# Cross-attention and quantised feed-forward: row sums added in two DMA chains, row maxima eight rows ahead, pair additions in two halves

## The reference

```python
xn = layer_norm(_layernorm(x), g1, b1);  cn = layer_norm(context, g2, b2)
q, k, v = xn @ Wq.T, cn @ Wk.T, cn @ Wv.T          # split into 16 heads of 32
scores = einsum('bqhs,bkhs->bhqk', q, k) / sqrt(32)  # masked with -inf
attn = softmax(scores, axis=-1)                     # over 2048 context rows
x = x + einsum('bhqk,bkhs->bqhs', attn, v) @ Wo.T + bo
z = _layernorm(x)                                   # then FP6 blocks of 32:
x = x + dequant(fp6(z)) @ dequant(fp6(weight)).T + bias
```

## Time and profile before

| | |
|---|---|
| time, median of 3 runs | 5028.72 us (5018.85 to 5039.0) |
| the profiled execution | 5029.38 us, span 5027.6 us |
| mean granted TensorE clock | 0.98 |
| busy share of the span | PE 93%, DVE 68%, ACT 57%, POOL 55% |

### The profile page before, as it was taken

The page is one execution under the profiler, slowest core; times in us unless marked ns, Lnnn a source line. Parts: engine busy times, 40 slices in busy tenths (PEclk is TensorE's granted clock), DMA queues, the critical chain, the costliest instruction groups (busy, mean ns, idle before and its releaser), DMA issues.

```text
span 5027.6 us, 65944 instructions
## 1 busy us (share of the span) xinstructions
PE 4669.9 (93%) x25616; PEld 1361.6 (27%) x25616; DVE 3425.6 (68%) x3983; ACT 2841.1 (57%) x5128; POOL 2761.9 (55%) x1218
## 2 busy tenths in 40 slices
PE   4999989998999989999899998999989999899998
PEld 2322242222422224222242222422224222242223
DVE  4688557885578855788557885568845788457883
ACT  3477634775347753477544774457744577446773
POOL 2267643676437663376633766346763467525665
PEclk9999999999999999999999999999999999999999
DMA  5223432234323343232432324323343223342232
GB/s 180 64 60 68 108 111 62 60 69 122 98 55 63 65 124 100 51 68 59 126 100 57 68 60 120 104 50 68 64 118 107 54 60 68 115 113 54 59 68 71
DMA packets 173787, 413.38 MB, mean 82 GB/s; under 512 B 26833, under 2 KB 100881, under 8 KB 146594
## 3 DMA queue, kind: packets, MB, share of 16 engines
q0 software_dynamic: 27648, 201.34, 19.9%
q1 hardware_dynamic: 145826, 207.83, 13.5%
HBM read 110.98 MB, written 21.01 MB: 26 GB/s over the span
## 4 chain that ended last, share of the span: by engine, by line
PE 73%; SPq 7%; DVE 6%; ACT 5%; DMA 4%; POOL 3%; issue 2%; ACTq 0%; DVEq 0%; POOLq 0%
PE banks L912 18%; PE banks L922 18%; PE banks L830 11%; PE banks L890 9%; PE banks L824 8%; PE banks L946 7%; SPq L286 4%; DVE max_parts L553 3%; ACT region L713 3%; SPq L312 3%; DMA queries_stacked<-max_rows 2%; PE banks L799 2%; POOL wkT_wvT_wqT L391 1%; DVE queries_stacked L578 1%; DMA region<-in_x 1%
## 5 line engine op out<-in xcount | busy, mean ns | idle before, releaser
L553 DVE TENSOR_REDUCE max_parts<-banks 128x2 f32<-128x1024 f32 x2048 | 2410.7, 1220 | 594.1 <-PE banks L890 592.0
L713 ACT ACTIVATE region<-banks 128x512 f32<-128x512 f32 x4096 | 2214.8, 595 | 830.5 <-PE banks L912 790.0
L391 POOL TENSOR_TENSOR wkT_wvT_wqT<-region 128x2048 f32<-128x2048 f32 x320 | 1474.6, 4608 | 1273.8 <-ACT region L713 1158.1
L912 PE MATMUL banks<-queries_stacked,keys_stacked 98*128 98x512 f16 x4096 | 1262.3, 388 | 90.3 <-DMA queries_stacked<-max_rows 57.6
L922 PE MATMUL banks<-region,values 128*32 128x512 f32 x8192 | 1105.3, 612 | 7.6
L890 PE MATMUL banks<-keys_stacked,queries_stacked 33*128 33x512 f16 x4096 | 661.7, 386 | 41.9 <-DMA keys_stacked<-region 33.1
L912 PEld LDWEIGHTS banks<-queries_stacked,keys_stacked 98*128 98x128 f16 x4096 | 277.7, 97 | 1433.0 <-ACT region L713 1262.4
L830 PE MATMUL banks<-region,wkT_wvT_wqT 128*128 128x512 f16 x2304 | 565.1, 386 | 50.4 <-POOL region L374 23.5
L571 DVE RECIPROCAL row_sums_inverse<-row_sums_inverse 128x128 f32<-128x128 f32 x256 | 235.3, 935 | 401.4 <-ACT row_sums_inverse L730 401.4
L544 DVE SCALAR_TENSOR_TENSOR region<-banks,region 128x512 f16<-128x512 f32 x192 | 132.5, 690 | 369.0 <-ACT region L698 368.1
L830 PE MATMUL banks<-wkT_wvT_wqT,region 128*128 128x512 f16 x1536 | 378.4, 390 | 1.2 <-DVE region L544 1.2
(11 more groups left out here) (77 smaller groups left out, 2793.0 us busy)
## 6 DMA issues: line engine op xcount, KB each, us to landing
wkT_wvT_wqT<-wkT_wvT_wqT POOLq DMA_DIRECT2D x128, 1024.0 KB, 7.0
wkT_wvT_wqT<-sums POOLq DMA_DIRECT2D x64, 1024.0 KB, 7.0
keys_stacked<-region SPq DMA_DIRECT2D x768, 64.0 KB, 2.0
region<-in_x SPq DMA_DIRECT2D x24, 1024.0 KB, 7.8
wkT_wvT_wqT<-weights_split SPq DMA_DIRECT2D x8, 3072.0 KB, 18.2
queries_stacked<-region SPq DMA_DIRECT2D x384, 64.0 KB, 2.0
region<-in_context SPq DMA_DIRECT2D x16, 1024.0 KB, 6.3
values<-in_context SPq DMA_DIRECT2D x16, 1024.0 KB, 6.0
```

The lines of the kernel that those rows point to most:

```text
L391: e.tensor_tensor(SUMS[dst], PR[i], PR[i + 1], ALU.add).then_inc(s_pr, 1)
L553: e.tensor_reduce(mpart[:, buf, :, a, t, c], MXB[parity], AX.X, ALU.max).then_inc(s_mxd, 1)
L713: e.activation(PR[u % 4][:, j * HALF:j * HALF + HALF], score_bank(kt, j)[0], ACT.Exp, scale=SCALE).then_inc(s_ex, 1)
L912: e.matmul(dst, KA[0:STR, ds(ka + (j * C + (u + 1) * P), P)], QA[0:STR, ds(qa[j], HALF)], start=True, stop=True).then_inc(s_st, 1)
```

## The change

- **Two chains.** The first chain adds pairs 1, 2, 3 onto pair 0 as before, but the buffers change their parts from unit to unit (`buffers`). A second chain adds pairs 5 and 6 onto pair 4 in `SUMS[4]` with two more DMAs (`merge_late`, semaphore `s_ac2`). In the last unit of a batch the second chain is left out.
- **Four row sums a unit** in place of six: `PR[2]` in step 15, and in the next unit `PR[3]` in step 0, the first chain in step 2, the second in step 5. The last unit has all six of its sources in step 15. ACT's copy of `LB` moves from tile 5 to tile 7, and three score banks are used from tile 8 on instead of from tile 6; there is no return to two banks at tile 15, but tile 0 has two.
- **Maxima eight rows ahead.** `HEAD` has eight rows of unit 1 instead of four, 48 half rows instead of 40, in the last 18 front entries instead of the last 16. The maxima are complete after step 7, the transposition stands inside step 9 and uses bank 4, and rows 8 to 15 of a unit are made one unit earlier.
- **Pairs in two halves.** Each addition on POOL is two instructions of 1024 columns; ACT waits for the half it needs.
- SP starts the load of the feed-forward weights one step later, directly before the loads of `x`.

```diff
-    HEAD = [(r, 0) for r in range(16)] + [(r, 1) for r in range(12, 16)]
-    DURING = dict(zip(FRONT[-16:], [3, 3, 3, 3] + [3, 3, 2, 0] + [3, 3, 3, 3] + [3, 3, 2, 0]))
+    HEAD = [(r, 0) for r in range(16)] + [(r, 1) for r in range(8, 16)]
+    NHEAD = len(HEAD)
+    DURING = dict(zip(FRONT[-18:], [2, 2] + [3, 3, 3, 3] + [3, 3, 2, 0] + [3, 3, 3, 3] + [3, 3, 3, 3]))
...
         def score_bank(tile, j):
-            if 6 <= tile < KT - 1:
-                return bank((7, 4, 5)[(4 * (tile - 6) + j) % 3]), 3
-            return bank(4 + j % 2), 2
+            if tile < 8:
+                return bank(4 + j % 2), 2
+            slot = 4 * (tile - 8) + j + ((tile, j) >= (10, 2))
+            return bank((7, 4, 5)[slot % 3]), 2 if tile == 10 and j >= 2 else 3
+        def buffers(n):
+            return [(0, 1, 2, 3, 4), (3, 1, 0, 2, 4), (2, 1, 3, 0, 4)][n % 3]
...
# SP
-                e.wait_ge(s_pv, b * (NU * KT) + NU * KT + 3)
+                e.wait_ge(s_pv, b * (NU * KT) + NU * KT + 4)
                 e.dma_start(SUMS[4], wd_dram).then_inc(s_fl, 16)
-                e.wait_ge(s_pv, b * (NU * KT) + NU * KT + 4)
                 for h in range(2):
                     e.dma_start(X1[:, 4 * h:4 * h + 4, :], xb[:, h]).then_inc(s_xl[h], 16)
...
# POOL
                         def pair(p, dst):
-                            e.wait_ge(s_ex, n * (KT * J) + (2 * p + 2) * J + 2)
                             i = 2 * (p % 2)
-                            e.tensor_tensor(SUMS[dst], PR[i], PR[i + 1], ALU.add).then_inc(s_pr, 1)
+                            for h in range(2):
+                                half = ds(2 * HALF * h, 2 * HALF)
+                                e.wait_ge(s_ex, n * (KT * J) + (2 * p + 1) * J + 2 * h + 4)
+                                e.tensor_tensor(SUMS[dst][:, half], PR[i][:, half], PR[i + 1][:, half],
+                                                ALU.add).then_inc(s_pr, 1)
+                        def merge_late(i, p, src):
+                            e.wait_ge(s_pr, n * 14 + 2 + 2 * (p + 1))
+                            if i > 0:
+                                e.wait_ge(s_ac2, (late + i) * 16)
+                            e.dma_start(SUMS[second], SUMS[src], accum_op=ALU.add).then_inc(s_ac2, 16)
...
+                        pair(0, first)
+                        if g + q > 0:
+                            e.wait_ge(s_ac2, (late - 1) * 16)
+                        pair(1, one)
+                        merge(0, 1, one)
+                        e.wait_ge(s_pv, n * KT + 4 + 3)
+                        pair(2, two)
+                        if g + q > 0:
+                            e.wait_ge(s_ac2, late * 16)
+                        pair(3, three)
+                        merge(1, 2, two)
+                        e.wait_ge(s_pv, n * KT + 4 + 6)
...
+                        pair(4, second)
+                        e.wait_ge(s_acc, (3 * n + 1) * 16)
+                        pair(5, one)
+                        merge(2, 3, three)
+                        if not end:
+                            merge_late(0, 5, one)
+                        pair(6, two)
+                        if not end:
+                            merge_late(1, 6, two)
...
# DVE, unit(g, q, last)
-                    for k in range(1, J - 1):
+                    if not end:
                         for t in range(QT):
-                            if not end:
-                                max_row(idx + 8 * k + 2 * t, 1 - q, k * QT + t)
-                            if last and k == J - 2:
-                                invert(m - 1, t)
-                        if last and k == J - 2:
-                            normalise(m - 1, n - 1)
-                    if not end:
-                        maxima(1 - q, n + 1, idx + 8 * (J - 1))
+                            max_row(idx + 8 + 2 * t, 1 - q, QT + t)
+                        maxima(1 - q, n + 1, idx + 16)
+                    if last:
+                        for t in range(QT):
+                            invert(m - 1, t)
+                        normalise(m - 1, n - 1)
                     if not last:
                         for t in range(QT):
-                            max_row(idx + 8 * (J - 1) + 2 * t, q, (J - 1) * QT + t)
+                            max_row(idx + 16 + 2 * t, q, 2 * QT + t)
+                        for t in range(QT):
+                            max_row(idx + 24 + 2 * t, q, 3 * QT + t)
                             if n > 0 and t >= 2:
                                 invert(m - 1, t - 2)
...
# ACT, unit(g, q, last)
-                            exps(m, g, kt // 4, kt % 4,
-                                 (lambda: row_sums(m - 1, KT + 4)) if kt == 5 and n > 0 else None)
...
+                            if kt == 7 and n > 0:
+                                halfway = lambda: row_sums(m - 1, KT + 6)
+                            if kt == 10 and not end:
+                                halfway = turned
+                            exps(m, g, kt // 4, kt % 4, halfway)
...
# PE, unit(g, q, last)
+                            if g + q > 0:
+                                if t == 0:
+                                    sums = [(PR[3], None)]
+                                if t == 2:
+                                    sums = [(SUMS[buffers(2 * g + q - 1)[0]], (s_acc, 48 * m))]
+                                if t == 5:
+                                    sums = [(SUMS[4], (s_ac2, 16 * (b * (2 * NU - 2) + 2 * (2 * g + q))))]
+                            step(m, ex, ka, qa, v, u, t + 1, rows[u], sums=sums, closing=t == 5,
+                                 between=(lambda: turn_next(ex)) if t == 9 and not end else None, turning=not end)
...
+                    quad(0, *at(0, 0, ng, nq, not end))
+                    quad(1, *at(1, 1, ng, nq, not end))
+                    quad(2, *at(2, 2, g + 1, q, not last))
                     ex, ka, v, rows = at(K3, J - 1, g + 1, q, not last)
```

More of the change, by code:

```diff
@@ L205, in build @@
         s_acc = sem("pairs_merged")
+        s_ac2 = sem("late_pairs_merged")
         s_po = sem("unit_outputs_done")
@@ L395, in merge @@
+                        first, one, two, three, second = buffers(2 * g + q)
+                        end = g == G - 1 and q == 1
+                        late = b * (2 * NU - 2) + 2 * (2 * g + q)
                         def merge(i, p, src):
-                            e.wait_ge(s_pr, n * 7 + 2 + p + 1)
+                            e.wait_ge(s_pr, n * 14 + 2 + 2 * (p + 1))
                             if i > 0:
                                 e.wait_ge(s_acc, (3 * n + i) * 16)
-                            e.dma_start(SUMS[here], SUMS[src], accum_op=ALU.add).then_inc(s_acc, 16)
@@ L403, in _ @@
-                        e.wait_ge(s_pv, n * KT + (3 if g + q > 0 else 4))
-                        pair(0, here)
-                        e.wait_ge(s_pv, n * KT + 4 + 2)
-                        pair(1, other)
-                        merge(0, 1, other)
-                        e.wait_ge(s_pv, n * KT + 4 + 4)
-                        pair(2, 2)
+                            e.dma_start(SUMS[first], SUMS[src], accum_op=ALU.add).then_inc(s_acc, 16)
+                        def merge_late(i, p, src):
+                            e.wait_ge(s_pr, n * 14 + 2 + 2 * (p + 1))
+                            if i > 0:
+                                e.wait_ge(s_ac2, (late + i) * 16)
+                            e.dma_start(SUMS[second], SUMS[src], accum_op=ALU.add).then_inc(s_ac2, 16)
@@ L410, in _ @@
+                        e.wait_ge(s_pv, n * KT + 4)
                         if n > 0:
                             e.wait_ge(s_acc, 3 * n * 16)
-                        pair(3, 3)
-                        merge(1, 2, 2)
-                        pair(4, other)
+                        pair(0, first)
[4 more added lines that the diff above has]
+                        e.wait_ge(s_pv, n * KT + 4 + 3)
@@ L909, in score @@
                             e.wait_ge(s_ex, ex + (u + 1) * J + j + 3 - back)
-                            if back == 3 and tile == 6 and j == 0:
+                            if tile == 8 and j == 0:
                                 e.wait_ge(s_on, m + 1)
+                            if tile == 11 and j == 0 and turning:
+                                e.wait_ge(s_mc, m + 2)
                             e.matmul(dst, KA[0:STR, ds(ka + (j * C + (u + 1) * P), P)],
@@ L932, in step @@
                             mm.then_inc(s_po, 1)
+                    if between:
+                        between()
                     score(2)
@@ L948, in step @@
                     mm.then_inc(s_pv, 1)
-                    if between:
-                        between()
                 def clear(bank, left, count):
@@ L982, in unit @@
                     clear(OB, s_oc, m + 1)
-                    quad(0, *at(0, 0, ng, nq, not end), *([[[c] for c in late(m - 1)]] if g + q > 0 else []))
-                    for k in range(1, K3):
```

(25 more changed lines are left out.)

69 lines of the change are left out of this document (34 added, 35 removed).

## The result

The changed kernel (called *after* below, the kernel before it *before*) took 5114.0 us (median of four runs, 5102.1 to 5127.0) against 5032.2 for before on the same chip: ratio 1.0166, 95% interval 1.0132 to 1.0201. It is slower by 1.7%; 4998 was forecast, 5042 was the upper end of the range. The profiled execution has a span of 5100.2 us, 72.6 above before's.

The account below looks back on a forecast made before the run. PE bounds the kernel, holding 73% of the span. Per batch -7.5 (units 1 to 5) - 1.4 (unit 0) - 7.1 (unit 6) + 1.5 (unit 7) + 3.0 (tail) + 7.6 (front) = -3.9, times eight -31: 4998 us, range 4936 to 5042.

Parts of the forecast that it names:

- The step that failed: POOL and new DMAs: pair 0 starts about 2 us late behind the second chain's transfers, priced at nothing.
- Rival 2: POOL's two halves hold DVE out as one; normalise 2.9 us late, 2.2 more in four units a batch: 5068; chance 0.09.
- Rival 3: Second chain lands late, PE's step 5 waits some 7 us in 48 units: +330, 5330; chance 0.03.
- Rivals 1 and 4: Rival 1: front not held up, 4934, chance 0.18; rival 4: no change, bounds met at upper ends, 5018, chance 0.13.
- unit 1, -1.78: Units 1 to 5, each: two row-sum sources -1.98, maxima wait -0.96, two-bank steps +1.16; bounds -2.94 and -1.2.
- the +0.35 for a late `normalise`: Units 2 to 5: normalise meets pair 1's first half, delaying row 2's reductions by 0.7, half covered; bounds 0 and 0.7.
- unit 6, -7.1: Unit 6: 54.50 us falls to 47.4, since maxima are joined after step 7; bounds -9 and -5.
- unit 7, +1.5: Unit 7: two row-sum sources moved behind the last outputs +1.0, two-bank steps +0.5; bounds 0 to 2.5.
- tail, +3.0: Tail: x becomes the second of two loads, behind the weights, and lands later; bounds 0 and 3.2.
- The front: Front: early reductions ahead of chunk 5's normalisation delay PE, +6.3, low clock +1.7, sum +7.6; bounds +4.5 and +10.
- -0.4 for the end of the front: Front's end: four more pairs hide the 1.43 wait and add 0.4 net; less low clock at unit 0, -0.8.
- The gain of 0.8 at unit 0's start: With the idle before unit 0 gone, its low clock may stay away: -0.8, half of 1.7.

Follow-up runs that it names:

- the kernel with the multiplication first: Changed kernel with GpSimd waiting for VectorE's normalise multiplication (of two units before) ahead of pair 1, except in unit 2: 5020.1 us, ratio to before 0.9981.
- the run with whole pairs: Changed kernel with each pair of tiles added in one POOL instruction again instead of two halves: 5098.7 us (one run).
- the kernels with the front's and with the tail's edit: Changed kernel with the last chunk normalised ahead of the early reductions: 5066.6 us; changed kernel with x loaded ahead of the feed-forward weights: 5097.9 us.

## Why the prediction was wrong

**The step that failed** is this one: "Pair 0 of the next unit starts behind that queue, about 2 us late, and ACT needs its buffers only in step 3. Cost nothing; without that cover every us of lateness is one us of PE in 48 units." Pair 0 was late by about that (2.1 us more in the long one of the two units shown), and in the kernel with the multiplication first POOL was as late and the units that have the wait took 47.2 to 47.4, so ACT had its buffers. But the price named one user of POOL's time and left out the other. The forecast let `normalise` meet the first half of pair 1 alone, with pair 1 starting when ACT has its exponentials ready; with pair 0 late, pair 1 is ready when pair 0 ends, and DVE waits for both halves. That cost 5.7 us in 15 units, 86 us. Without it after would have come out near 5028, within half a per cent of before and inside the range; the front's 2.4 us a batch over its forecast are 19 of the 30 that then remain.

**Rival 2** had the mechanism ("it decides once POOL's second half is queued before the first ends") and was given 0.09. It was dismissed by the earlier trace rows, where DVE was through at once between two POOL operations. There the next operation began 0.04 us before the last one ended; in the long units it is 0.3. The row didn't show the case in question. Its price was too low (2.2 a unit: the clock was left out, and it takes two halves, not one), its number too high (32 units; 15 met it).

The Trainium skill's rule that was cited (SBUF — State Buffer, section Who interferes with whom: whole instructions exclude each other, issue order decides) agrees with the rows in part: DVE gets in at a boundary between two additions only where the second hasn't begun yet. The longest that the runs show of this is 18 us (below).

**Rival 3** did not come: the first late merges took 11.4 to 13.8 us in place of 7.0, and PE never waited for them. **Rivals 1 and 4** fall with the front and the long units.

**What was right, step by step** (us a batch, predicted and measured against before, long units aside): unit 1, -1.78 and 49.3 to 47.4 = -1.9; units 2 to 5, -1.43 each and 49.3 (their median before) to 47.83 = -1.5; the +0.35 for a late `normalise` in it, and 0.33 by the run with whole pairs; unit 0, -1.4 and -1.5; unit 6, -7.1 and 54.4 (its median before) to 47.7 = -6.7; unit 7, +1.5 and +1.9; tail, +3.0 and +2.7.

**The front** was right in its mechanism and short in its size: +7.6 forecast, +10.0 measured. The hold-up with its clock was put at 8.0, and undoing it gave back 6.3. What remains over before is 3.7, where the forecast had -0.4 for the end of the front. Eight pairs more stand in a front, at 0.39 us 3.1 of these; the forecast counted the four at its end at 0.4 net of a hidden wait. PE's wait for the stacked copies grew a little (4.84 at 826.08, 4.05 in the earlier trace rows; 36.8 in all, 33.1 in before), and the clock is low behind it (0.50 from 827 to 831; 0.57 from 804 to 808 in the earlier trace rows). How the 3.7 divide among these was not tested. The gain of 0.8 at unit 0's start was not found.

**Open**: what makes the first late merge land later in 15 of 40 units than in the other 25, at the same place in the code. In the 15 it lands 6.07 us or more after the unit's first score, in the 25 at most 5.88. It isn't chance: all 15 are long again in the kernels with the front's and with the tail's edit (17 and 16 long units). The trace has a companion, transfers of 8 or 16 KB on the DMA queues that the page calls `instruction` (packets, MB, share of 16 engines):

```profile
q8 instruction: 195, 3.19, 0.3%
q14 instruction: 121, 0.99, 0.1%
```

Between the issue of the first chain's last merge and the landing of the first late one, such a transfer runs in all 15 long units and in 16 of the others; the nine merges without one land within 11.37 to 11.41 us, those with one in 11.36 to 13.76. That these transfers are the cause was not tested. What is shown, by the merge sent 2.3 us earlier, is that the overlap of the two merges makes up most of what the late one takes beyond 7.0 (8.5 in place of 11.4).

## What to carry to other kernels

When an engine's work is shifted by a stated time, price it for every engine that shares something with it, not only for the one that waits on its result: here 2 us on GpSimd were free for ScalarE and cost 86 us by way of a multiplication of 0.69 us on VectorE. Look for such short instructions that must fall into a gap of another engine, and make the gap by a semaphore (0.74 us of GpSimd's idle time) rather than leave it to timing. In a unit mean that moves little, look for two populations before pricing anything by the mean.

## What was unexpected of the hardware

A VectorE multiplication can be shut out by a row of GpSimd instructions as long as each begins before the last one ends. Timeline of after, unit 7 of the third batch: it lasts from 1855.57 to 1873.63, through additions and DMA issues. There are two such in after, and they cost nothing: unit 7 takes 51.68 us in all eight batches. The kernel in which each half waits for the last one has none of these.

```profile
1855.57 18.06 DVE L604 TENSOR_TENSOR queries_stacked<-queries_stacked,row_sums_inverse 128x512 f32<-128x512 f32 x1
1857.02 1.18 POOL L410 DMA_DIRECT2D sums<-wkT_wvT_wqT  x1
1857.63 5.27 POOL L399 TENSOR_TENSOR wdT<-region 128x1024 f32<-128x1024 f32 x2
1862.26 5.25 POOL L399 TENSOR_TENSOR wkT_wvT_wqT<-region 128x1024 f32<-128x1024 f32 x2
1866.88 1.48 POOL L410 DMA_DIRECT2D sums<-wkT_wvT_wqT  x1
1867.50 5.57 POOL L399 TENSOR_TENSOR wkT_wvT_wqT<-region 128x1024 f32<-128x1024 f32 x2
```

And a later start can be faster: two steps' delay of GpSimd's pair 0 gained 88 us of span over after, because pair 0 then came out of a wait and not from a DMA issue. In after's trace, a half that began before a DMA issue ahead of it had ended always overlapped the next half by over 0.1 us in the record (187 of 187), and one behind a wait of over 0.1 us never did (235).
